# Reordering the SyncE queue's transfers at the start of a two-layer gated cross-attention kernel

## The reference

```
x = x + tanh(g_xattn[0]) * attention0(layernorm(x), ctx)   # 16 heads of 8, causal mask, then W_o and b_o
x = x + tanh(g_ffn[0])   * experts0(layernorm(x))          # 6 low-rank experts, top 1
x = x + tanh(g_xattn[1]) * attention1(layernorm(x), ctx)   # 8 heads of 64
x = x + tanh(g_ffn[1])   * experts1(layernorm(x))          # router per batch, 2 of 8 experts, then a layer norm
```

## Time and profile before

| what | us |
|---|---|
| median of 3 runs | 201.99 |
| lowest and highest | 201.96 and 204.09 |
| the profiled execution's own time | 202.17 |
| its span in the profile | 200.2 |

### The profile page before, as it was taken

How to read it: one execution, slowest core, us unless ns; L and a number is a source line. 1 busy time by engine, 2 the same in 40 slices (tenths; PEclk the granted TensorE clock), 3 DMA queues, 4 the chain that set the end, 5 groups by cost and what they waited for, 6 DMA issues and landing times.

```text
span 200.2 us, 4350 instructions
## 1 busy us (share of the span) xinstructions
PE 179.6 (90%) x1516; PEld 128.7 (64%) x1516; DVE 139.2 (70%) x361; ACT 121.7 (61%) x313; POOL 105.3 (53%) x153
## 2 busy tenths in 40 slices
PE   0799898799999999999799997999999988999990
PEld 0588353245456667477577775867867777989980
DVE  1584697878888456728857899488688584766844
ACT  0557502656598867857976696598689754155240
POOL 7402000282565637865884788858955846253232
PEclk9999999999999999999999999999999999999998
DMA  5969998960000300000000000000240007808101
GB/s 122 322 180 232 234 187 232 186 104 0 8 0 5 102 10 0 0 3 0 0 3 3 3 0 0 0 3 0 84 157 0 2 8 232 236 4 239 50 0 52
DMA packets 14744, 15.04 MB, mean 75 GB/s; under 512 B 1695, under 2 KB 12164, under 8 KB 14724
## 3 DMA queue, kind: packets, MB, share of 16 engines
q1 hardware_dynamic: 13676, 14.28, 27.5%
q10 hardware_dynamic: 1048, 0.50, 1.0%
HBM read 10.98 MB, written 3.67 MB: 73 GB/s over the span
## 4 chain that ended last, share of the span: by engine, by line
PE 64%; DVE 15%; ACT 5%; DMA 5%; POOL 3%; issue 3%; SPq 2%; POOLq 0%; ACTq 0%; DVEq 0%
PE PS L1258 7%; PE PS L1287 7%; PE PS L1271 7%; PE PS L1329 7%; DVE MX L754 6%; PE PS L1319 5%; PE PS L1135 4%; PE PS L1299 4%; DMA POOLED<-qk_scr 3%; PE PS L1092 3%; PE PS L1244 3%; PE PS L1097 2%; PE PS L1033 2%; SPq L352 2%; DMA X<-in_x 2%
## 5 line engine op out<-in xcount | busy, mean ns | idle before, releaser
L458 POOL TENSOR_TENSOR POOLED<-POOLED,RC 128x512 f32<-128x512 f32 x32 | 33.4, 1063 | 6.6 <-DVE RC L866 6.5
L650 ACT ACTIVATE POOLED<-PS,NM 128x256 f32<-128x256 f32 x64 | 29.5, 479 | 6.6 <-DVE NM L857 6.0
L754 DVE TENSOR_REDUCE MX<-PS 128x4 f32<-128x1024 f32 (+1 forms) x24 | 28.3, 1219 | 5.8 <-PE PS L1097 5.6
L447 POOL TENSOR_SCALAR_AFFINE_SELECT PT<-PT 128x512 f32<-128x512 f32 x16 | 10.2, 637 | 37.4 <-ACT PT L570 37.1
L570 ACT ACTIVATE PT<-PS 128x768 f32<-128x768 f32 x32 | 25.2, 810 | 5.2 <-PE PS L1116 3.6
L857 DVE TENSOR_REDUCE NM<-PS 128x4 f32<-128x1024 f32 x16 | 19.4, 1218 | 3.8 <-PE PS L1258 3.7
L415 POOL TENSOR_SCALAR VE<-MV 128x2 f32<-128x2 f32 x20 | 5.5, 273 | 29.2 <-DVE MV L707 15.8
L681 ACT ACTIVATE POOLED<-PS,BI 128x256 f32<-128x256 f32 x32 | 12.5, 475 | 9.8 <-PE PS L1319 8.0
L1258 PE MATMUL PS<-KT,VA 64*128 64x256 f32 x128 | 17.3, 397 | 0.4 <-ACT VA L638 0.4
L1271 PE MATMUL PS<-CST,POOLED 128*128 128x128 f32 x128 | 16.6, 275 | 0.0
L1287 PE MATMUL PS<-POOLED,V 128*64 128x256 f32 x128 | 16.0, 387 | 0.5 <-DVE POOLED L873 0.5
(11 more groups left out here) (146 smaller groups left out, 382.0 us busy)
## 6 DMA issues: line engine op xcount, KB each, us to landing
POOLED<-in_w SPq DMA_DIRECT2D x8, 512.0 KB, 4.1
POOLED<-qk_scr SPq DMA_DIRECT2D x8, 384.0 KB, 6.5
qk_scr<-POOLED SPq DMA_DIRECT2D x8, 192.0 KB, 3.6
qk_scr<-POOLED SPq DMA_DIRECT2D x8, 128.0 KB, 2.4
W<-in_w SPq DMA_DIRECT2D x3, 256.0 KB, 6.0
BI<-in_bias SPq DMA_DIRECT2D x8, 66.0 KB, 4.3
qk_scr<-POOLED SPq DMA_DIRECT2D x8, 64.0 KB, 4.4
out_x<-X SPq DMA_DIRECT2D x4, 128.0 KB, 1.8
```

What stands on the lines that cost most here:

```text
L458: g_.tensor_tensor(pr, pr, RC1[:, n % 2, 2 * h:2 * h + 2].unsqueeze(2).to_broadcast([P, 2, S]), ALU.mult).then_inc(s_p1p, 1)
L650: last = a.activation(PR[n % 3][:, h, it, :], pair("sc", n)[:, h * 512 + it * S:h * 512 + (it + 1) * S], ACT.Exp, bias=NM1[:, n % 2, 2 * h ...
L754: v.tensor_reduce(MX0[:, b, it, :, hw * k:hw * (k + 1)], pair("S", n).rearrange("p (r h j) -> p r h j", r=2, h=hw), AXX, ALU.max, negate=T ...
```

## The change

It permutes entries of SP_ORDER and touches nothing else.

```
 SP_ORDER = table("""
-x:0 x:1 w0 c:0 x:2 c:1 w1:1 w1:2 c:2 so:0:0 so:0:1 so:0:2 so:1:0 so:1:1 si:0 so:1:2 wo:0 so:2:0 vec si:1 so:2:1
-so:2:2 so:3:0 one so:3:1 so:3:2 shift:0 si:2 si:3 shift:1 shift:2 shift:3 w1:0 wo:1 w12:0 w12:1 w12:2 w12:3
+x:0 x:1 w0 c:0 x:2 c:1 w1:1 w1:2 c:2 so:0:0 so:0:1 so:0:2 si:0 so:1:0 so:1:1 so:1:2 si:1 so:2:0 so:2:1 so:2:2
+so:3:0 one so:3:1 vec so:3:2 shift:0 si:2 wo:0 si:3 shift:1 shift:2 shift:3 w1:0 wo:1 w12:0 w12:1 w12:2 w12:3
 outd:0 outd:1 outd:2 outd:3
 """)
```

## The result

The changed kernel took 208.52 us (median of 4 runs, 206.38 to 209.68) against 202.01 for the kernel before: a ratio of 1.0261, 95% interval 1.0138 to 1.0384. I had forecast 203.4, slower but within 1%, and a range up to 204.9. Measured again later on one chip with other kernels it was 1.0350 (1.0319 to 1.0381). Ratios compare means and leave out runs more than 1.5% above the fastest of the same kernel; here these runs are mostly those whose clock was low for longest, so a ratio can understate what the medians show. The profiled execution is the fastest of its four, 206.38 us with a span of 204.4.

A forecast was written before the change was run, and what follows sets the result against it. Time is won or lost only before about 45 us, where TensorE waits for transfers. -0.6 at S:0, given back at S:6, and +1.4 at S:12 on 202.17 gave 203.6, as median 203.4; range 201.3 to 204.9.

The forecast's parts named there:

- si:0 earlier: Start of SyncE's list: si:0 issued 0.95 us earlier, S:0 from 23.06 to some 22.45, a gain of 0.6.
- so:1 behind si:0: so:1 lands later, si:1 released 1.0 us later at 24.2; S:0's 0.6 is waited away at S:6, price 0.
- What stands behind si:1: SyncE takes 10.6 us from si:1 to shift:0; shift:0 and si:2 go out 2.4 later, S:12 1.4 late.
- The two delays don't add: T:0:0's is smaller: T:0:0's delay lies ahead of S:12 on TensorE and is smaller, so only S:12's 1.4 us counts.
- The sum: -0.6 at S:0, given back at S:6, +1.4 at S:12: 203.6 profiled, 203.4 as median.
- +1.4: Price in us of S:12 starting late on TensorE because si:2 lands late; bounds 0.9 to 4.1.
- C: Rival: deeper backlog, si:2 slower or so:1 keeping si:1 until 25; S:12 +2.1 to +4.1, middle 204.8; chance 0.21.
- B: Rival: so:1 shares the engines with si:0, si:1 issued at 21 to 22, start gain kept; 201.3; chance 0.14.
- D: Rival: no effect, S:12's delay absorbed by later slack or S:0's 0.6 kept; say 202.3; chance 0.13.
- vec and wo:0: Both issued later on SyncE but landing before GpSimd reads vec at 39.96 and wo:0's first read at 55.90; price 0.
- the queue is served in the order of issue: SyncE's transfers are served about in issue order, si at 175 KB/us, so and the loads at 316 KB/us (an estimate).

The follow-up runs named there:

- si:0 alone: The kernel before with only si:0 moved ahead of so:1:0 and so:1:1; 205.41 us, ratio 1.0073.
- the fill: The changed kernel plus ten useless matmuls on TensorE ahead of T:0:0's wait for shift:0; 204.41 us, against 209.50 for the change beside it.
- shift:0 early: The changed kernel with shift:0 moved ahead of so:3:1, vec and so:3:2; 206.46 us, ratio 1.0198.
- the mixture: The kernel before with si:0 between so:1:0 and so:1:1, shift:0 ahead of so:3:1, vec behind so:3:1, wo:0 behind si:2; 205.22 us, ratio 1.0139.
- so:2:0 back: The changed kernel with so:2:0 ahead of si:1 again; four runs from 202.87 to 208.56 us, no ratio.
- TensorE's list altered: The changed kernel with T:0:0 and T:0:1 behind S:10 and S:11 on TensorE, SyncE's list untouched; 208.67 us, ratio 1.0312.
- fewer bytes: The changed kernel with so:2:0 and so:3:0 writing one plane of three, 512 KB less; four runs from 202.87 to 209.08 us, no ratio.
- both deadlines relieved: The changed kernel with shift:0 and si:2 both ahead of so:3:1, vec and so:3:2; 203.66 us, ratio 1.0068.
- so:2:0 alone: The kernel before with only so:2:0 moved behind si:1; 205.49 us, ratio 1.0119.

## Why the prediction was wrong

**si:0 earlier: right in the mechanism.** 0.8 us earlier, landing at 15.3+6.5 = 21.8; S:0 no longer waits. In the first profile it gained 0.17 us and not 0.6: TensorE ended kv:1:1 at 22.90 there, 0.5 later than before, so its own work covered the rest. In the second measurement's profile S:0 began at 21.79, 1.3 us earlier than before. What S:0 gains depends on TensorE's own work, and one trace didn't give its spread.

**so:1 behind si:0: right for the change.** I put the release of si:1 at 24.2, and it was 23.83; S:6 at 31.4, and it began at 31.68. One term in between was wrong: with nothing queued ahead of it, si:1's second DMA took 7.4 us to land and not 6.5. That S:6 loses nothing held only because nothing was issued in the wait for si:1; with si:0 alone moved, it waited 2.6 us.

**What stands behind si:1: the step that failed first.** I had 10.6 us from si:1 to shift:0. It was 13.0 in the first profile and 11.9 in the second. The eight so:2 and so:3:0 took 6.7 us and not 4.2, the rest of so:3 with vec 3.9 and not 3.1, `one` 1.6 and not 2.5. I had carried over the durations of the earlier trace rows entry by entry, from a list in which so:2:0 stood ahead of si:1. shift:0 thus left at 36.8 and not at 34.8, was there 2.7 us later, and T:0:0 started 3.6 us late and not 1.4.

**"The two delays don't add: T:0:0's is smaller": the wrong path.** The order of my two deadlines was turned round. T:0:0 decided, by way of the maxima and T:2:0, and S:12 (45.56) found si:2 landed a microsecond earlier (37.9+6.6 = 44.5). With the fill it was the same: T:0:0 2.2 us late, S:12 without a wait. The deadline of S:12 was real, but as the next one, as the kernel with shift:0 early shows.

**The sum: a term was missing.** What TensorE's idle time does to the time that follows I put at nothing, without a reason: 5.1 us of the 7.1 between the kernel before and the changed one in the second measurement went away with the fill, while T:0:0 stayed as late. I had the row for it, the granted clock of the earlier trace rows, only at full speed, and never asked what a wait of 1.4 to 3 us on TensorE in mid-kernel would do to it. Without the clock's part, my "+1.4" compares with 1.7 us of span, or 1.0% by the runs. That late transfers behind si:1 cost time was right. That the size came so near is partly luck, for it came by T:0:0 and not by S:12, and in the first profile the late T:0:0 alone was worth 3.6 us.

**The rivals.** C had the right direction and the right kind of places, though si:2 took its 6.6 us and so:1 didn't keep si:1 until 25; its 204.8 was too low, for it had no price for the clock either. B and D fell. vec and wo:0 were priced rightly at nothing. That the queue is served in the order of issue held only roughly. so:1 landed behind si:0, at 22.1 to 23.8 against 21.85. But the first two DMAs of so:2, issued behind si:1 at 24.67 and 25.14, took 6.3 us each and landed at 31.0 and 31.4, ahead of si:1's second at 31.6. A later transfer may complete before an earlier one, as the Trainium skill says (DMA: Bandwidth & Descriptors, Queues, rings and completion order), and this trace agrees.

## What to carry to other kernels

A DMA issued while its queue's engine would otherwise wait costs that engine no time; behind that wait it delays everything behind it. It may still hold up the transfers under way, as with si:0 alone. So look at which later waits such an entry stands in front of, and how much each has to spare (here 1.3 us for si:2 at S:12), and at when its own data are ready before you move it ahead (shift:0 in the mixture). When a change can leave TensorE idle for some microseconds in mid-kernel, price the clock beside the wait: with transfers as late, the kernel took 204.4 us at full clock and 209.5 with the clock falling. And let ten useless matmuls in the wait, as a test, tell the two prices apart.

## What the runs showed of the hardware that I had not expected

TensorE's granted clock fell to 0.50 in traces with a wait in mid-kernel: after 3.2 us idle (for 3.4 us, the change), 2.6 (3.4 us, si:0 alone), 2.0 (3.4 us, shift:0 early, at S:12), 2.1 (near 7 us, so:2:0 back), 2.2 (13 us, TensorE's list altered), 2.6 (13 us, fewer bytes), 2.9 (13 us, the change again). It did not fall after a wait of 1.1 us in the kernel with both deadlines relieved, nor after 1.4 us in the profiled run of the mixture, nor with 0.5 us left by the fill. The length of the low stretch does not follow the length of the wait, and TensorE's work in it did not end it soon: in the second measurement of the change it was busy for 11.99 of 12.70 us and still at 0.50. In the kernel with so:2:0 alone, 1.8 us of idle at T:0:0 left the clock at 1.00, and 1.4 us more, up to 44.24, was followed by the fall:

```profile
36.10:37.90 1.80, 0.00 (x0) 0.00 (x0) 1.23 (x1) 0.52 (x1) 0.00 (x0) 1.00 0.34 81
38.00:43.00 5.00, 3.94 (x56) 1.74 (x56) 2.98 (x4) 3.92 (x6) 2.89 (x7) 1.00 1.01 175
43.00:44.20 1.20, 0.00 (x0) 0.00 (x0) 0.00 (x0) 0.71 (x1) 1.20 (x3) 1.00 1.08 177
44.50:51.00 6.50, 6.50 (x50) 1.99 (x48) 3.67 (x3) 1.64 (x3) 1.36 (x3) 0.50 0.41 66
```

And one issue of so's DMAs (L352) on SyncE took from 0.36 to 2.4 us, the longest in the kernel with so:2:0 alone, just behind si:1. With 512 KB less in the queue the stretch from si:1 to shift:0 was no shorter.
